# One source tile per chunk of a graph network layer: columns copied on chip by VectorE and ScalarE in place of one gather

## What is computed

```python
h = relu(layernorm(x))
m = relu(concat([h[src], h[dst], edge_attr]) @ w1 + b1) @ w2 + b2   # one message per edge
agg = segment_sum(m, dst, num_segments=12500)
gi, gh = agg @ w_ih + b_ih, h @ w_hh + b_hh                         # split in r, z, n
r, z = sigmoid(gi_r + gh_r), sigmoid(gi_z + gh_z)
n = tanh(gi_n + r * gh_n)
out = x + (1 - z) * n + z * h
```

## Time and profile before

| what | us |
|---|---|
| median of 3 runs (4000.51 to 4002.24) | 4001.66 |
| the profiled execution, its own time | 4009.54 |
| its span, first to last instruction | 4007.8 |
| POOL busy | 2991.4 (75%) |
| PE busy | 2996.9 (75%) |
| DVE busy | 1716.2 (43%) |
| ACT busy | 1281.7 (32%) |

### The profile page before, as it was taken

How to read it: one execution, slowest core, us unless ns; L and a number is a source line. 1 busy time by engine, 2 the same in 40 slices (tenths; PEclk the granted TensorE clock), 3 DMA queues, 4 the chain that set the end, 5 groups by cost and what they waited for, 6 DMA issues and landing times.

```text
span 4007.8 us, 76313 instructions
## 1 busy us (share of the span) xinstructions
PE 2996.9 (75%) x20157; PEld 2691.1 (67%) x20157; DVE 1716.2 (43%) x6014; ACT 1281.7 (32%) x3575; POOL 2991.4 (75%) x3163
## 2 busy tenths in 40 slices
PE   5777777777777777777777777777777777777777
PEld 4667666667666666666666667666666666766666
DVE  6444444444444444444444444444444444444443
ACT  5333333333333323333333333333333333333332
POOL 4777777777777777777777777777777777777776
PEclk8888889888888888888888888888888888888887
DMA  6222222222222222222222222222222222222222
GB/s 187 68 69 69 69 69 69 69 69 70 69 69 69 70 70 69 69 69 70 69 69 69 69 69 70 69 69 69 70 69 69 69 69 69 69 69 69 69 69 56
DMA packets 275619, 287.99 MB, mean 72 GB/s; under 512 B 153847, under 2 KB 204696, under 8 KB 275475
## 3 DMA queue, kind: packets, MB, share of 16 engines
q0 software_dynamic: 100000, 205.00, 20.4%
q1 hardware_dynamic: 147282, 69.63, 6.1%
q10 hardware_dynamic: 28318, 13.14, 1.2%
HBM read 274.60 MB, written 12.83 MB: 72 GB/s over the span
## 4 chain that ended last, share of the span: by engine, by line
POOL 71%; issue 26%; DMA 1%; POOLq 1%; DVE 1%; PE 1%; ACT 0%; SPq 0%; DVEq 0%; ACTq 0%
POOL rows L423 71%; POOLq L227 1%; DMA p_rows<-low 1%; POOLq L238 0%; DMA acc<-in_x_dram 0%; DVE stats L700 0%; PE ps L1032 0%; PE ps L1005 0%; DVE mv L706 0%; DVE dst_int L779 0%; DMA onehot<-base_f_dram 0%; DVE low L725 0%; PE ps L1093 0%; PE ps L1094 0%; ACT low L505 0%
## 5 line engine op out<-in xcount | busy, mean ns | idle before, releaser
L423 POOL DMA_INDIRECT rows<-p_rows,idx x3125 | 2960.9, 947 | 964.4 <-issue 952.3
L574 ACT ACTIVATE lhs<-ps 96x640 f32<-96x640 f32 x625 | 437.6, 700 | 2590.5 <-PE ps L1008 2585.4
L1032 PE MATMUL ps<-onehot,rows 128*128 128x95 f32 x6250 | 915.1, 298 | 427.0 <-ACT rows L580 425.9
L1032 PEld LDWEIGHTS ps<-onehot,rows 128*128 128x128 f32 x6250 | 830.6, 210 | 520.9 <-ACT rows L580 290.4
L800 DVE TENSOR_TENSOR rows<-rows,ps 128x640 f32<-128x640 f32 x625 | 512.7, 820 | 1341.3 <-DMA rows<-p_rows,idx 1335.2
L1019 PE MATMUL ps<-rhs,lhs 128*128 128x128 f32 x6250 | 983.8, 315 | 68.9 <-DVE rows L800 68.4
L1019 PEld LDWEIGHTS ps<-rhs,lhs 128*128 128x128 f32 x6250 | 919.0, 229 | 97.2 <-issue 89.9
L1005 PE MATMUL ps<-ident,onehot 128*96 128x128 f32 x3125 | 547.6, 315 | 475.0 <-DVE onehot L790 473.8
L1005 PEld LDWEIGHTS ps<-ident,onehot 128*96 128x96 f32 x3125 | 385.6, 145 | 567.7 <-DVE onehot L790 560.2
L790 DVE TENSOR_SCALAR onehot<-iota_w,dst_int 128x95 f32<-128x95 f32 x3125 | 736.1, 298 | 51.1 <-issue 51.0
L580 ACT ACTIVATE rows<-rows 128x640 f32<-128x640 f32 x625 | 460.0, 736 | 84.6 <-DVE rows L800 82.1
(11 more groups left out here) (94 smaller groups left out, 1307.9 us busy)
## 6 DMA issues: line engine op xcount, KB each, us to landing
rows<-p_rows,idx POOLq DMA_INDIRECT x3125
lhs<-in_ea_t_dram SPq DMA_DIRECT2D x625, 80.0 KB
idx<-in_src_cols_dram SPq DMA_DIRECT2D x625, 2.5 KB
p_rows<-low SPq DMA_DIRECT2D x14, 448.0 KB, 3.6
x_fin<-in_x_dram ACTq DMA_DIRECT2D x123, 50.0 KB
out_dram<-out_fin ACTq DMA_DIRECT2D x123, 50.0 KB
acc<-in_x_dram SPq DMA_DIRECT2D x13, 448.0 KB, 4.8
low<-in_dst_rows_dram SPq DMA_DIRECT2D x1, 1562.5 KB
```

The costliest lines, as they stand in the source:

```text
L423: pool.indirect_dma_start(out=rows[:, s, t, :], out_offset=None, in_=p_rows[:, :], in_offset=bass.IndirectOffsetOnAxis(ap=idx[:, s, t:t + ...
L574: nc.scalar.activation(lhs[0:WB, s, :], onehotT_ps, ACT.Copy, accum_out=count[:, s:s + 1])
L1032: nc.tensor.matmul(sg[:, 0:W], rows[:, s, t, :], onehot[:, s, t, 0:W], start=(t == 0), stop=(t == T - 1))
```

## The change

Tile 24 of each chunk, the last of group 4, is no longer gathered, so group 4 has four gathers. The 128 source columns of that tile are copied one by one out of `hT` into a new tile `picked`, whose column e is the column of the node of edge e. DVE copies the first 64 and ACT the other 64, 16 in each of the slots 1 to 4. The node numbers are loaded at setup (`pick_nat`), turned into 16-bit numbers on DVE (`pick_half`) and laid as two long rows into `low` by two SP transfers. Each part of 16 begins with one TENSOR_LOAD of 16 numbers into registers. PE then adds `picked` times `w1_keep` (a copy of the source weight) onto the fifth matmul of group 4 in PSUM. The add of group 4 on DVE and its relu on ACT cover four tiles, and a relu straight from PSUM (`relu_direct`) makes the fifth.

```diff
@@ SP, before the first sums @@
+                    sp.wait_ge(ranges_ready, 1)
+                    sp.wait_ge(w2ih_copied, 2)
+                    for half, row in enumerate((pick_dve, pick_act)):
+                        sp.dma_start(row.rearrange("o (c e) -> o c e", e=HALF),
+                                     pick_half[0:CHUNKS, half * HALF:(half + 1) * HALF]).then_inc(pick_in, 16)
+                    sp.wait_ge(pick_in, 32)
@@ POOL @@
-                    for t in range(T):
+                    for t in range(gather_tiles(s)):
@@ ACT (DVE has the same with pick_dve, nc.vector.tensor_copy and e = k * PICK + j) @@
+            def pick_columns(c, k):
+                if k == 0:
+                    act.wait_ge(pick_in, 32)
+                    wait(act, pre_ready[LAST], c)
+                _, nodes = nc.values_load_multi_w_load_instructions(
+                    pick_act[0:1, bass.ds(c * HALF + k * PICK, PICK)], (mybir.EngineType.Activation,), min_val=0, max_val=N - 1,
+                    skip_runtime_bounds_check_because=IN_RANGE)
+                for j, node in enumerate(nodes):
+                    e = HALF + k * PICK + j
+                    last = nc.scalar.copy(picked[:, e:e + 1], hT[:, bass.ds(node, 1)])
+                last.then_inc(picked_act, 1)
+
+            def relu_direct(c):
+                act.wait_ge(pre_ready[LAST], c + 1)
+                wait(act, seg_ready[LAST], c)
+                nc.scalar.activation(rows[:, LAST, T - 1, :], pre_ps[LAST % 2][:, (T - 1) * D:T * D], ACT.Relu).then_inc(direct_ready, 1)
@@ ACT, chunk @@
                     copy_onehot(c, s)
+                    old = before(c, s, 1)
+                    if s == 0 and old:
+                        relu_direct(old[0])
...
                         relu_message(*old)
+                    if s >= PICK_FROM:
+                        pick_columns(c, s - PICK_FROM)
@@ PE, pre_activation @@
                 if old:
 
                     pe.wait_ge(summed[old[1]], old[0] + 1)
+                    if s == 0:
+                        pe.wait_ge(direct_ready, old[0] + 1)
...
+                    if direct:
+                        pe.wait_ge(picked_dve, (c + 1) * PICKS)
+                        pe.wait_ge(picked_act, (c + 1) * PICKS)
+                        last = nc.tensor.matmul(pre_ps[s % 2][:, t * D:(t + 1) * D], picked[:], w1_keep[:], start=False, stop=True)
```

More of the change, by code:

```diff
@@ L10 @@
 I32 = mybir.dt.int32
+U16 = mybir.dt.uint16
 P = 128
@@ L53, with gather_tiles @@
 LN = LAG * FN
+PICKED_TILE = G * T - 1
+HALF = P // 2
+PICK = 16
+PICKS = HALF // PICK
+PICK_FROM = G - PICKS
+LAST = G - 1
+IN_RANGE = "src holds node indices, 0 to N - 1"
+def gather_tiles(s):
+    return T - 1 if s == LAST else T
 D = 128
@@ L104, in gnn_kernel @@
         at += GROUPS
+        pick_nat = low[:, at:at + P].bitcast(I32)
+        at += P
+        pick_half = low[:, at:at + HALF].bitcast(U16)
+        at += HALF
         assert at <= NPAD
+        pick_dve = low[2 * ED:2 * ED + 1, 0:CHUNKS * HALF // 2].bitcast(U16)
+        pick_act = low[3 * ED:3 * ED + 1, 0:CHUNKS * HALF // 2].bitcast(U16)
         dst_int = sb("dst_int", [P, GROUPS * T], I32)
@@ L115, in gnn_kernel @@
         w1_dst = sb("w1_dst", [P, D])
+        w1_keep = sb("w1_keep", [P, D])
+        picked = sb("picked", [P, P])
         idx = sb("idx", [P, G, T], I32)
@@ L211, in gnn_kernel @@
         fin_chain = sem("fin_chain")
+        pick_in, picked_dve, picked_act, direct_ready = (sem(n) for n in (
+            "pick_in", "picked_dve", "picked_act", "direct_ready"))
         g_zeroed, g_mask_set, g_scattered, g_chain, g_b1_in = (sem(n) for n in ("g_zeroed", "g_mask_set", "g_scattered", "g_chain", "g_b1_in"))
         g_h_ready, g_q_ready, g_q_copied, g_q_stored = (sem(n) for n in ("g_h_ready", "g_q_ready", "g_q_copied", "g_q_stored"))
-        g_src_in, g_dst_in, g_ea_in = (sem(n) for n in ("g_src_in", "g_dst_in", "g_ea_in"))
+        g_src_in, g_dst_in = (sem(n) for n in ("g_src_in", "g_dst_in"))
         g_gathered = sems("g_gathered", 3)
-        g_bc_ready, g_bcT_ready, g_pre_ready, g_summed, g_message_ready, g_seg_ready, g_new_ready = (sem(n) for n in (
-            "g_bc_ready", "g_bcT_ready", "g_pre_ready", "g_summed", "g_message_ready", "g_seg_ready", "g_new_ready"))
+        g_bc_ready, g_bcT_ready, g_new_ready = (sem(n) for n in ("g_bc_ready", "g_bcT_ready", "g_new_ready"))
+        g_ea_in, g_pre_ready, g_summed, g_message_ready, g_seg_ready = (v[0] for v in (
+            ea_in, pre_ready, summed, message_ready, seg_ready))
         g_sums_in, g_sumsT_ready, g_sumsT_kept = (sem(n) for n in ("g_sums_in", "g_sumsT_ready", "g_sumsT_kept"))
@@ L309, in load_indices @@
             def load_indices(c, s):
-                wait(sp, rows_in[s], c * (16 * T))
+                wait(sp, rows_in[s], c * (16 * gather_tiles(s)))
                 sp.dma_start(idx[:, s, :], src_cols[bass.ds(c * (G * P) + s * P, P), :]).then_inc(idx_in[s], 16)
@@ L645, in fast @@
                 over_chunks(act, chunk)
+                relu_direct(CHUNKS - 1)
                 for back in (2, 1):
@@ L793, in build_onehot, with pick_columns @@
                 last.then_inc(onehot_ready[s], 1)
+            def pick_columns(c, k):
+                if k == 0:
+                    dve.wait_ge(pick_in, 32)
+                    wait(dve, pre_ready[LAST], c)
+                _, nodes = nc.values_load_multi_w_load_instructions(
+                    pick_dve[0:1, bass.ds(c * HALF + k * PICK, PICK)], (mybir.EngineType.DVE,), min_val=0, max_val=N - 1,
+                    skip_runtime_bounds_check_because=IN_RANGE)
+                for j, node in enumerate(nodes):
+                    e = k * PICK + j
+                    last = nc.vector.tensor_copy(picked[:, e:e + 1], hT[:, bass.ds(node, 1)])
+                last.then_inc(picked_dve, 1)
             def add_pre(c, s):
+                k = gather_tiles(s)
                 dve.wait_ge(pre_ready[s], c + 1)
-                dve.wait_ge(rows_in[s], c * (16 * T) + 16 * T)
-                r = rows[:, s, :, :].rearrange("p t f -> p (t f)")
-                nc.vector.tensor_tensor(r, r, pre_ps[s % 2], ALU.add).then_inc(summed[s], 1)
+                dve.wait_ge(rows_in[s], c * (16 * k) + 16 * k)
+                r = rows[:, s, 0:k, :].rearrange("p t f -> p (t f)")
+                nc.vector.tensor_tensor(r, r, pre_ps[s % 2][:, 0:k * D], ALU.add).then_inc(summed[s], 1)
             def add_segments(c, s, prev):
@@ L1025, in segment_sums @@
                 pe.wait_ge(message_ready[s], c + 1)
+                if s == LAST:
+                    pe.wait_ge(direct_ready, c + 1)
                 old = before(c, s, 1)
```

18 lines of the change are left out of this document (11 added, 7 removed).

## The result

The kernel after takes **5693.07 us** (median of 4 runs, 5688.96 to 5697.11) against 4001.95 (4000.51 to 4002.27) for the kernel before on the same chip: ratio **1.423**, 95% interval 1.420 to 1.425. Forecast were 4360 us and a range of 4060 to 5500. The sign was right, the size was not, and the time lies outside the range.

What follows compares the result with a forecast made beforehand. POOL's gathers bound the kernel before at 31.26 us per chunk; after, the circle binds: A 8.27, B 8.00, C 6.55, D 10.6, plus 0.7 clock, is 34.1 us. That adds 355 us, plus 3 for setup: 4360 us, range 4060 to 5500.

Steps and rivals of the forecast that it cites:

- the circle: Longest way round the engines waiting for each other, without row waits: 28.0 us per chunk before, against POOL's 31.26.
- The copies: 16 one-column copies per part in slots 1 to 4: 1.6 us on ACT, 2.1 us on DVE.
- The loads: One TENSOR_LOAD of 16 numbers ahead of each part's copies, on ACT and DVE: assumed 1.0 us each.
- A: From PE's gates to `candidate_pre` on DVE: 6.31 us before, 8.27 us with slot 3's ACT part.
- B: From `candidate_pre` to the next chunk's onehot tiles: 8.00 us with slot 4's ACT part between relu and tanh.
- D: From slot 1's onehot tiles to the next gates: 9.44 us before, 10.6 us with DVE's slot 1 part.
- C: Slot 0, onehot to onehot: 6.20 us before, plus 0.35 us for `relu_direct` and PE's added matmul, 6.55 us.
- The clock: PE's steps on the way round slowed by the granted clock of 0.87: up to 1.4 us per chunk, 0.7 taken.
- 33.4 + 0.7 = 34.1 us: Forecast time per chunk: the four pieces' sum plus the clock allowance, above POOL's 30.01 us with 24 gathers.
- The rival of dear loads: Loads from 1.6 us each are the main cost: 4920 us, or 5745 at 16 full prices; chance 0.32.
- DVE copies that block POOL: Each of DVE's 64 copies stops POOL, which then needs 35.3 to 38.4 us per chunk: 4510 to 4910; chance 0.05.
- Faster: Rival that the copies vanish in the slack of all engines' way round: 3845 to 3990 us; chance 0.12.

Runs made afterwards that it cites:

- e12: Kernel before without the last gather of group 4 from the second chunk on, nothing in its place: 3847.7 us, ratio 0.9615.
- e16: e10 with `relu_direct` in slot 0 moved behind the window copy and the relu of the gathered tiles: 4353.9 us, ratio 1.088.
- e10: Kernel after with the two index rows kept as 32-bit instead of 16-bit numbers, at the same partitions: 4646.2 us, ratio 1.161.
- e14: Kernel after with ACT's parts moved behind the sigmoids and the tanh, 16-bit loads kept: 5448.7 us.
- e9: Kernel after with unused transposes added on PE where it waits for onehot tiles: 5617.8 us.
- e13: Kernel after with 32-bit loads, ACT's parts and `relu_direct` behind, uneven parts (DVE 8, 24, 20, 12; ACT 8, 16, 20, 20): 3844.6 us, ratio 0.9605.

## Why the prediction was wrong, step by step

- **POOL bound before, with a slack of 3.3 us on the circle.** Right as far as it was shown. e12 gains 154 us, so the slack is at least 1.25 us. The 3.3 us themselves rest on the sum, whose steps e16 bears out.
- **The copies, 1.6 and 2.1 us a part.** Right: 16 copies take 1.58 us on ACT and 1.88 on DVE.
- **The loads, 1.0 us.** This is the step that failed. They are 3.56 and 3.81 us. The term was marked as an assumption, priced by the 43 to 53 ns of a register step. The trace of before had loads of one number only, a 32-bit one, and the 32-bit form comes near that price (59 ns per further number, 1.20 and 1.32 us for the whole). The diff, however, makes 16-bit rows, and a further 16-bit number costs 184 ns or more; that the type might matter wasn't weighed. By e10 this term is worth 1047 us, 8.4 us per chunk. The prediction's own rule, 3 x 125 us for each further us of load, would have given 3 x 2.7 = 8.1 us. So where the loads fall on the circle was right, and their size was not.
- **A 8.27, B 8.00, D 10.6.** With loads near the assumed size they are 8.51, 8.17 and 10.76. Right. One remark behind them held for such loads only: that DVE's own part fits in its wait for the sigmoids. With loads of 3.8 us DVE's queue is a second way round, 23.5 us long (e14).
- **C 6.55: `relu_direct` for 0.35 us.** Wrong in mechanism. It was priced as its own duration plus the added matmul. It waits for the whole pre-activation of its group, and the window copy and the big relu stand behind it on ACT: moving it gives back 292 us, 2.4 us per chunk (e10 to e16). At 2.4 us this is the second step that failed.
- **The clock, 0.7 us.** It fell from 0.87 to 0.73. That is no term to be added: where the circle runs through PE, as in slot 0, the lower level costs some 2 us (C is 7.42 in the first chunk of e9 and 9.60 in the kernel after); where DVE's queue runs beside it nothing (e9).
- **33.4 + 0.7 = 34.1 us.** Near e16 (33.99), which is the kernel after with 32-bit loads and the relu moved. That the two agree to 0.1 us is in part luck: in e16 A, B and C are 0.2, 0.1 and 0.35 us longer than predicted, with loads 0.2 to 0.3 us longer than assumed, and this fills the place of the 0.7 us for the clock. The kernel after is 34.0 + 2.4 for the early relu + 8.4 for the loads = 44.8; each of these is the difference of two runs that differ in that one thing.
- **The rival of dear loads** was given 0.32 up to 5745 us. Its mechanism is the right one. Its value at 16 full prices, 45.2 us per chunk, is near the measured 44.75 by luck: those loads would be 4.6 and 4.9 us, and the rest of the difference is C. The range ended at 5500 since only loads were in its upper part. The measured loads put into the prediction's sum give 34.1 + 2 x 2.6 + 2.8 = 42.1 us, about 5360, still inside; the 2.4 us of the early relu took the time out of it.
- **The rule of the Trainium skill** ("Runtime: NRT & Kernel Launch", section "Instruction fetch mechanics", about 200 ns per register even in bulk) gave 3.3 us a load. The page speaks of registers loaded from HBM, and these loads read on-chip memory. For this kernel's 16-bit loads the trace agrees all the same: (3556 - 287) / 15 = 218 ns on ACT. For 32-bit loads it does not: (1197 - 287) / 15 = 61 ns. Had the rule been taken for the sum, 5225 us would have stood there, still 470 short, mostly for C.
- **DVE copies that block POOL.** Not seen: the gathers are 946 ns.
- **Faster.** Only with three changes (32-bit loads, the parts and the early relu moved behind, uneven parts), as e13.

## What to carry to other kernels

An engine that is idle more than half of its time, as DVE here, can still have hardly any room: add up the way round, then add each new instruction in program order, and ask of each wait what stands behind it in its engine's queue. An operand that the trace has never shown in this form (here 16 adjacent 16-bit numbers into registers) must be priced by its worst row, or measured first. Once a gain is lost, it may still be had by moving the work into waits that exist: the same 128 copies with their loads cost 42% in one place and form, and nothing in another.
